# Ten products of the identity with itself on TensorE ahead of each unit's first attend, in the second of three attention stages

## The chip, the cores and the metric

The kernel runs on one core of one Trainium2 chip. The metric is the device time of one launch in microseconds; of several runs the median counts.

## The reference

Two layers on 128 sequences of 128 x 256 values. What matters here, cut from the reference:

```python
# layer 0: grouped convolutions of x and of the context, attention over 8 heads, layernorm
qh, kh, vh = _gconv(q, wq), _gconv(k, wk), _gconv(v, wv)
scores = jnp.einsum('bhdl,bhdm->bhlm', qh, kh) / sqrt(H) - 1000000000.0 * mask
...
# layer 1: self attention, cross attention with the context, feed forward
attn1 = _mha(x, x, x, look_ahead_mask, ...)
out1 = _layernorm(x + attn1, ln1_g, ln1_b)
attn2 = _mha(enc_output, enc_output, out1, padding_mask, ...)
out2 = _layernorm(out1 + attn2, ln2_g, ln2_b)
ffn = jax.nn.relu(out2 @ ffn_w1 + ffn_b1) @ ffn_w2 + ffn_b2
return _layernorm(out2 + ffn, ln3_g, ln3_b)
```

with, in each `_mha` (16 heads of depth 16),

```python
logits = jnp.einsum('bhqd,bhkd->bhqk', qh, kh) / jnp.sqrt(depth) + mask * -1000000000.0
attn = jax.nn.softmax(logits, axis=-1)
out = jnp.einsum('bhqk,bhkd->bhqd', attn, vh)
```

## The kernel before, in words

Four stages run one after the other: the convolution attention (tiles named l_), the first attention of layer 1 (mha_), the second one (mha_ too), and the feed forward (ffn_). The change touches the function `attention` (line 387), which builds the first three; its argument `phase` is 0, 1 or 2, and `PLANS[phase]` (line 52) holds the table of numbers by which each stage's work is set in slots. The second stage is `phase == 1`: 32 units (`N`) of four sequences, 512 tokens.

A unit has 16 attend steps, one for each slot, and each works on four heads of one sequence (four quads of heads for each of four sequences). In slot `i` TensorE computes, in this order (`body`, line 862):

- `attend_step(t, i)` (line 789), the first thing in each slot: four products (line 807) of keys with queries, 128 x 128 each, into `tbank[i % 2]` (banks 4 and 5 of PSUM). The operands are stacks of bf16 rows: 96 rows of split keys or queries, and three rows that carry the row maxima, so that the product comes out with the maximum of the row subtracted. For a unit's first half the maxima must have arrived before slot 0, for the second before slot 8: `max_in[0]` and `max_in[1]` are raised by the DMA that brings them.
- `pv_tile` (line 813): the probabilities of four slots times the values, 32 small-column products (line 821 in the profile) for the two slots' worth of each of four steps.
- `score_step` (line 765, products on line 775): scores of the *next* unit in the other orientation, whose only use is the row maximum. VectorE takes it (line 1076) from two banks in turn.
- the work of the table `work`: projections (line 740), values (line 759), the turn of the maxima (`max_turn`, line 780, products on line 784) and of the output (line 858).
- `output_step`, `turn_merged`, `turn_heads` (lines 852, 839, 832): the end of each sequence of the unit.

The way of the maxima: VectorE's maxima of eight score steps, GpSimd's split into three bf16 parts (line 1227), TensorE's two transposes (line 784: in slot 13 for the first half of the next unit, in slot 5 for the second half of this one), ScalarE's copy (line 924), and a DMA from ScalarE's queue into the stack (line 926). The first attend of the unit, in slot 0, waits for it.

After an attend step VectorE adds the mask in the bank (line 1091), and ScalarE takes the exponent (line 936), which frees the bank and raises `att_exp`. The attend step of slot `i` needs the exponent of slot `i - 2`:

```python
                if i % 8 == 0:
                    pe.wait_ge(max_in[i // 8], 16 * (u.u + 1))
                    if u.number() == 0 and i == 0:
                        pe.wait_ge(ones_in, ONES)
                wait(pe, att_exp, CHUNKS * u.u + i - 1)
```

All engines run orders that are written out by these tables; waits are semaphores, and each engine takes its instructions in order. `c["identb"]` is the 128 x 128 identity in bf16, made once at the start (line 312) and used as the operand of the max transposes.

Of the kernel before, what the change touches and what calls it, by code (L numbers as in the profile page):

```python
# [28 lines left out]
P = 128  # L29
# [3 lines left out]
CHUNKS = 16  # L33
# [17 lines left out]

PLANS = (
    dict(
        score=[3, 4, 5, 7, 7, 8, 10, 10, 11, 12, 12, 13, 14, 15, 16, 18],
        pv_lag=2,
        steps={'turn': 6, 'normalise': 10},
# [14 lines left out]
        split_slot=14,  # L71
    ),
    dict(
        score=[4, 6, 7, 7, 8, 9, 11, 12, 12, 13, 13, 14, 15, 15, 17, 18],
        pv_lag=2,
        steps={'turn': 6, 'turn_merged': 7, 'output': 8, 'normalise': 10},
# [16 lines left out]
        split_slot=13,  # L93
    ),
    dict(
        score=[3, 3, 5, 6, 6, 8, 9, 10, 11, 12, 12, 14, 14, 16, 17, 17],
        pv_lag=1,
        steps={'turn': 5, 'turn_merged': 7, 'output': 8, 'normalise': 9},
# [44 lines left out]
def wait(eng, sem, value):  # L143

    if isinstance(value, int) and value <= 0:
        return
    eng.wait_ge(sem, value)
# [239 lines left out]
def attention(nc, top, c, io, phase):  # L387
# [32 lines left out]
    with ExitStack() as ctx:  # L420
# [5 lines left out]
        def sem(n):  # L426
            if n not in signals:
                signals[n] = top.enter_context(nc.semaphore(f"{('even', 'odd')[phase % 2]}_{n}"))
            return signals[n]
# [62 lines left out]
        work, sbank, tbank, pvbank, fbank = bank[0:2], bank[2:4], bank[4:6], bank[6], bank[7]  # L492
# [17 lines left out]
        att_mm, att_masked, att_exp, att_pv = sem("att_mm"), sem("att_masked"), sem("att_exp"), sem("att_pv")  # L510
# [38 lines left out]
        def place(side, h):  # L549

            return 2 * h + side if conv else H * side + 2 * (h % 8) + h // 8
# [14 lines left out]
        plan = PLANS[phase]  # L566
# [146 lines left out]
        def _(pe):  # L713
# [74 lines left out]

            def attend_step(u, i):
                j, q, kt = ATT[i]  # L790
                if i % 8 == 0:
                    pe.wait_ge(max_in[i // 8], 16 * (u.u + 1))
                    if u.number() == 0 and i == 0:
                        pe.wait_ge(ones_in, ONES)
                wait(pe, att_exp, CHUNKS * u.u + i - 1)
                key = ((j // KT) * KT + kt) * P
                masked = i in plan["pe_masks"]
                if masked:
                    if u.number() == 0:
                        pe.wait_ge(c["masks_ready"], c["masks_parted"])  # L800
                    for part in range(2):
                        mask = c["mask0t_parts"][:, part, kt, (j % 2) * P:(j % 2 + 1) * P]
                        nc.tensor.matmul(tbank[i % 2][:, :].rearrange("p (s l) -> p s l", s=4), c["ident_r"][:, :],
                                         mask.unsqueeze(1).to_broadcast([P, 4, P]), start=part == 0, stop=False)
                for s in range(4):
                    h = 4 * q + s
                    mm = nc.tensor.matmul(tbank[i % 2][:, s * P:(s + 1) * P],  # L807
                                          stack[0:STACKED, u.par, place(1, h), key:key + P],
                                          stack[0:STACKED, u.par, place(0, h), j * P:(j + 1) * P],
                                          start=not masked, stop=not masked or s == 3)  # L810
                mm.then_inc(att_mm, 1)
# [50 lines left out]
            def body(t):  # L862
                for slot in range(16):
                    if exists(t, N):
                        attend_step(t, slot)
                    for at in products_in(t, slot):
                        pv_tile(*at)
                    for u, i in scores_in(t, slot):
                        score_step(u, i)
                    for u, what, step, piece, pieces in banks.in_slot(t, slot):  # L870
                        bank_ = work[banks.bank(what, step)]
                        if piece == 0:

                            wait(pe, work_out, banks.free(u, what, step))
                        if what == "project":
                            project_step(u, step, bank_, piece, pieces)
                        elif what == "values":
                            value_step(u, step, bank_, piece, pieces)
                        elif what == "max":
                            max_turn(u, step, bank_)  # L880
                        else:
                            turn_y(u, step, bank_)
                    if not conv:
                        for at in finish_in(t, slot, "output"):
                            output_step(*at)
                        for at in finish_in(t, slot, "turn_merged"):
                            turn_merged(*at)
                    for at in finish_in(t, slot, "turn"):
                        turn_heads(*at)
# [720 lines left out]
```

## Time and profile before

| | us |
|---|---|
| median of 3 runs | 4573.87 |
| the runs | 4562.73, 4573.87, 4581.44 |
| the profiled execution | 4555.99 |
| its span, first to last instruction | 4554.0 |
| TensorE busy | 4138.1 (91%) |
| VectorE busy | 3630.7 (80%) |
| ScalarE busy | 3142.2 (69%) |
| GpSimd busy | 3055.6 (67%) |
| granted TensorE clock, mean | 0.977 of 2.4 GHz |

The span begins with the first instruction and ends with the last; 2 us lie around it. A matmul's busy time in the profile has its way through the array in it, so that four products in a row, each on record with 0.22 us, take 0.24 us together. The second stage lies between about 1657 and 2766 us of the span. The granted clock is given as a share of full speed: 1.00 is 2.4 GHz, 0.50 is 1.2 GHz, and a value between is a mean over a stretch that holds both.

### The profile page before, as it was taken

The page shows a single profiled execution, that of the slowest core. Times are in us where ns is not written, and L with a number is a line of the kernel's source. Part 1 is how long each engine was busy: PE and PEld are TensorE (multiplying, and loading weights), DVE is VectorE, ACT ScalarE, POOL GpSimd, SP SyncE. Part 2 cuts the span into 40 slices and gives each one's busy share as a digit, 9 for nine tenths or more (in the row PEclk, how much of TensorE's full clock was granted, in tenths as well). Part 3 has the DMA queues.
Part 4 walks back from the last instruction along what each step waited for, and adds up shares of the span by engine and source line. Part 5 has one row for each costly group of instructions (what it writes and reads, how often), then busy time and mean ns, then how long its engine had stood idle before and what let it go on. Part 6 is the DMA issues. An engine that isn't in the chain of part 4 may idle for free. (4 is left out here: it accounts for less than half of the span.)

```text
span 4554.0 us, 131241 instructions
## 1 busy us (share of the span) xinstructions
PE 4138.1 (91%) x46088; PEld 3382.9 (74%) x46088; DVE 3630.7 (80%) x13903; ACT 3142.2 (69%) x6279; POOL 3055.6 (67%) x4630
## 2 busy tenths in 40 slices
PE   7999999999999969998999986999999997999999
PEld 5777777777777747777777764778777876999998
DVE  7898888889889858888888884777777775666666
ACT  5777777777777748777777774777777775444443
POOL 4777777777777637777777763777777773555555
PEclk9999999999999989999999997999999998999999
DMA  5444444444444435556656554667767662222221
GB/s 142 117 120 121 119 122 117 119 121 118 123 117 120 111 102 154 157 151 159 163 150 168 158 143 122 182 193 193 194 195 197 193 183 93 73 75 70 70 70 52
DMA packets 1082968, 608.89 MB, mean 134 GB/s; under 512 B 64665, under 2 KB 1082057, under 8 KB 1082313
## 3 DMA queue, kind: packets, MB, share of 16 engines
q1 hardware_dynamic: 1071896, 595.70, 47.7%
q8 instruction: 370, 6.06, 0.6%
q10 hardware_dynamic: 10416, 4.80, 0.4%
q14 instruction: 286, 2.34, 0.2%
HBM read 175.66 MB, written 117.54 MB: 64 GB/s over the span
## 5 line engine op out<-in xcount | busy, mean ns | idle before, releaser
L1076 DVE CUSTOM_DVE_ANT_0 l_junk<-l_bank,mask 128x256 bf16<-128x256 f32 x2048 | 775.4, 416 | 57.5 <-PE l_bank L775 38.1
L936 ACT ACTIVATE mha_probs<-mha_bank 128x512 f32<-128x512 f32 x1024 | 602.3, 599 | 222.6 <-DVE mha_bank L1091 114.6
L936 ACT ACTIVATE l_probs<-l_bank 128x512 f32<-128x512 f32 x1024 | 598.8, 592 | 161.8 <-DVE l_bank L1091 149.1
L1091 DVE TENSOR_TENSOR l_bank<-l_bank,mask0t 128x512 f32<-128x512 f32 x832 | 572.3, 688 | 16.5 <-PE l_bank L807 8.1
L1076 DVE CUSTOM_DVE_ANT_0 mha_junk<-mha_bank,mask 128x128 bf16<-128x128 f32 x2048 | 464.8, 284 | 45.3 <-PE mha_bank L775 44.8
L775 PE MATMUL mha_bank<-mha_stack 96*128 96x128 bf16 (+1 forms) x4096 | 373.1, 222 | 72.8 <-DVE mha_max_parts L1076 51.0
L807 PE MATMUL mha_bank<-mha_stack 99*128 99x128 bf16 (+1 forms) x4096 | 403.9, 223 | 27.8 <-DMA mha_stack<-mha_max_rows 26.4
L807 PE MATMUL l_bank<-l_stack 99*128 99x128 bf16 x4096 | 402.9, 220 | 23.9 <-ACT l_probs L936 16.2
L1445 ACT ACTIVATE ffn_hidden<-ffn_h,ffn_b_s 128x512 f32<-128x512 f32 x256 | 176.5, 689 | 356.1 <-PE ffn_h L1392 284.9
L775 PE MATMUL l_bank<-l_stack 96*128 96x256 bf16 x2048 | 374.9, 275 | 30.9 <-DVE l_max_parts L1076 25.5
L1405 PEld LDWEIGHTS ffn_o<-ffn_w_parts,ffn_hidden_parts 128*128 128x128 f32 x3072 | 384.9, 191 | 14.9 <-DVE ffn_w_parts L1516 3.5
L1091 DVE TENSOR_TENSOR mha_bank<-mha_bank,mask1t 128x512 f32<-128x512 f32 x512 | 353.6, 691 | 52.6 <-PE mha_bank L807 52.1
L1462 DVE TENSOR_TENSOR ffn_hidden_parts<-ffn_hidden,ffn_hidden_parts 128x512 fp32r<-128x512 f32 x256 | 242.1, 946 | 190.9 <-ACT ffn_hidden_parts L1445 190.6
L1405 PE MATMUL ffn_o<-ffn_w_parts,ffn_hidden_parts 128*128 128x256 f32 x3072 | 388.2, 283 | 4.7 <-DVE ffn_w_parts L1516 3.1
L1392 PE MATMUL ffn_h<-ffn_x_parts,ffn_w_parts 128*128 128x512 f32 x1536 | 374.6, 393 | 14.9 <-DVE ffn_x_parts L1457 14.3
L807 PEld LDWEIGHTS l_bank<-l_stack 99*128 99x128 bf16 x4096 | 280.4, 99 | 143.8 <-issue 83.4
L1218 POOL TENSOR_TENSOR mha_yproj<-mha_yproj,mha_parts 128x512 f32<-128x512 f32 x248 | 290.3, 1170 | 138.8 <-ACT mha_parts L909 138.6
L1067 DVE TENSOR_REDUCE mha_max_parts<-mha_bank 128x4 f32<-128x512 f32 x512 | 335.8, 681 | 36.5 <-PE mha_bank L775 34.4
L807 PEld LDWEIGHTS mha_bank<-mha_stack 99*128 99x128 bf16 (+1 forms) x4096 | 291.1, 99 | 95.0 <-DMA mha_stack<-mha_max_rows 36.6
L775 PEld LDWEIGHTS mha_bank<-mha_stack 96*128 96x128 bf16 (+1 forms) x4096 | 254.0, 98 | 140.0 <-DVE mha_max_parts L1076 63.1
L1224 POOL TENSOR_TENSOR mha_parts<-mha_yproj,mha_parts 128x512 bf16<-128x512 f32 x248 | 288.6, 1164 | 71.3 <-ACT mha_parts L978 70.3
L1392 PEld LDWEIGHTS ffn_h<-ffn_x_parts,ffn_w_parts 128*128 128x128 f32 x1536 | 282.3, 190 | 69.4 <-issue 15.7
(192 smaller groups left out, 11266.8 us busy)
## 6 DMA issues: line engine op xcount, KB each, us to landing
mha_stack<-mha_parts SPq DMA_DIRECT2D x1536, 128.0 KB, 2.9
l_stack<-l_parts SPq DMA_DIRECT2D x1024, 64.0 KB
l_stack<-l_parts SPq DMA_DIRECT2D x256, 128.0 KB
cols_o<-mha_y_t SPq DMA_DIRECT2D x128, 256.0 KB, 3.0
l_x_pad<-in_x SPq DMA_DIRECT2D x64, 256.0 KB, 3.3
l_c_pad<-in_ctx SPq DMA_DIRECT2D x64, 256.0 KB, 3.7
l_resid<-in_x_t SPq DMA_DIRECT2D x64, 256.0 KB, 3.1
cols_x<-l_y SPq DMA_DIRECT2D x64, 256.0 KB, 2.4
```

What stands on the lines that cost most here:

```text
L775: mm = nc.tensor.matmul(sbank[i % 2][:, s * KEYS:(s + 1) * KEYS], stack[0:SCORED, u.par, place(0, h), j * P:(j + 1) * P], stack[0:SCORED, ...
L807: mm = nc.tensor.matmul(tbank[i % 2][:, s * P:(s + 1) * P], stack[0:STACKED, u.par, place(1, h), key:key + P], stack[0:STACKED, u.par, pla ...
L936: nc.scalar.activation(probs[:, i % RING, :], tbank[i % 2][:, :], ACT.Exp).then_inc(att_exp, 1)
L1067: nc.vector.tensor_reduce(max_parts[:, j, 0, col:col + SH * GROUPS - 1:GROUPS], sbank[i % 2][:, :].rearrange("p (s k) -> p s k", s=SH), op ...
L1076: ins = nc.vector.tensor_tensor_reduce(out=junk[:, i % 2, cols], in0=sbank[i % 2][:, cols], in1=mask, scale=1.0, scalar=LOWEST, op0=ALU.ad ...
L1091: nc.vector.tensor_tensor(bank_, bank_, mask.unsqueeze(1).to_broadcast([P, 4, P]), ALU.add).then_inc(att_masked, 1)
L1218: nc.gpsimd.tensor_tensor(rest, rest, parts[:, u.par, i, HI, :], ALU.subtract).then_inc(rest_step, 1)
L1224: nc.gpsimd.tensor_tensor(parts[:, u.par, i, LO, :], rest, parts[:, u.par, i, MID, :], ALU.subtract).then_inc(split_done, 1)
L1392: mm = nc.tensor.matmul(hbank[f % 4][:, :], w1_parts[:, a, kt, f * P:(f + 1) * P], x_parts[:, u.par, b, kt, :], start=(i == 0), stop=(i == 5))
L1405: mm = nc.tensor.matmul(obank[j][:, 0:L], hidden_parts[:, u.par, b, f, j * P:(j + 1) * P], w2_parts[:, a, f, :], start=(f == 0 and i == 0) ...
L1445: last = nc.scalar.activation(out, hbank[f % 4][:, :], ACT.Relu, bias=c["ffn_b1_s"][:, f:f + 1])
L1462: nc.vector.tensor_tensor(hidden_parts[:, u.par, 1, f, :], hidden[:, f % 2, :], hidden_parts[:, u.par, 0, f, :], ALU.subtract).then_inc(h_ ...
```

## The change

The plan of each stage gets an entry `rehearsals`, a pair: how many extra products stand ahead of the attend step in slot 0 and in slot 8. It is (10, 0) in the second stage and (0, 0) in the others. Each product is the bf16 identity (stationary) with the bf16 identity (moving), 128 columns, written into the bank that the attend step fills right after. It goes to the four column groups of the bank in turn. The attend's products overwrite all of it, so no result uses them. The wait for the exponent that frees the bank moves ahead of the extra products, and with that ahead of the wait for the maxima, in all three stages.

```diff
@@ -71,6 +72,7 @@
     dict(
+        rehearsals=(10, 0),
         score=[4, 6, 7, 7, 8, 9, 11, 12, 12, 13, 13, 14, 15, 15, 17, 18],
@@ -788,11 +791,14 @@
             def attend_step(u, i):
                 j, q, kt = ATT[i]
+                wait(pe, att_exp, CHUNKS * u.u + i - 1)
                 if i % 8 == 0:
+                    for n in range(plan["rehearsals"][i // 8]):
+                        nc.tensor.matmul(tbank[i % 2][:, (n % 4) * P:(n % 4 + 1) * P], c["identb"][:, :],
+                                         c["identb"][:, :], start=True, stop=True)
                     pe.wait_ge(max_in[i // 8], 16 * (u.u + 1))
                     if u.number() == 0 and i == 0:
                         pe.wait_ge(ones_in, ONES)
-                wait(pe, att_exp, CHUNKS * u.u + i - 1)
                 key = ((j // KT) * KT + kt) * P
```

In TensorE's order, at the boundary between the first and the second unit of the second stage (last rows of slot 15, then slots 0 and 1), there stands before:

```order
L858 MATMUL mha_bank<-ident,mha_z 128x128
L839 MATMUL mha_bank<-ident,mha_merged 128x128 [waits odd_merged_done]
L839 MATMUL mha_bank<-ident,mha_merged 128x128
L807 MATMUL mha_bank<-mha_stack 128x128 [waits odd_att_exp,odd_max_in0]
L807 MATMUL mha_bank<-mha_stack 128x128 x3
L858 MATMUL mha_bank<-ident,mha_z 128x128 [waits odd_normed,odd_work_out]
L858 MATMUL mha_bank<-ident,mha_z 128x128
L852 MATMUL mha_bank<-mha_wo,mha_merged_t 128x256 [waits odd_mt_out]
```

and with the change, at the same place (three lines further down in the code up to the attend step, six behind it: 807 is now 813, 858 is 864, 839 is 845, 852 is 858):

```order
L864 MATMUL mha_bank<-ident,mha_z 128x128
L845 MATMUL mha_bank<-ident,mha_merged 128x128 [waits odd_merged_done]
L845 MATMUL mha_bank<-ident,mha_merged 128x128
L797 MATMUL mha_bank<-identb 128x128 [waits odd_att_exp]
L797 MATMUL mha_bank<-identb 128x128 x9
L813 MATMUL mha_bank<-mha_stack 128x128 [waits odd_max_in0]
L813 MATMUL mha_bank<-mha_stack 128x128 x3
L864 MATMUL mha_bank<-ident,mha_z 128x128 [waits odd_normed,odd_work_out]
```

The ten products of line 797 stand between the end of the old unit and the first attend, and the one row that waited for two semaphores is now two rows that wait for one each. This piece comes 31 times; in the first unit of the stage the ten have no wait. Nothing else moves on any engine.

## Rows read from the trace of the kernel before

**Rows 1.** Page, 40 equal slices of the span: granted TensorE clock in tenths.

```profile
PEclk9999999999999989999999997999999998999999
```

**Rows 2.** Stretches of stages 2 and 3: length, busy time (instructions) by engine, clock, DMA.

```profile
1700.00:2735.00 1035.00, 943.45 (x10907) 753.61 (x10905) 894.63 (x5051) 804.21 (x1612) 745.01 (x1032) 0.96 0.59 156
2834.00:3799.00 965.00, 894.04 (x11478) 763.62 (x11477) 752.74 (x1665) 727.24 (x1441) 726.56 (x806) 1.00 0.67 186
```

**Rows 3.** Waits of TensorE, 1685 to 2780 us: total us, times, longest.

```profile
PE mha_bank L807 <- DMA mha_stack<-mha_max_rows: 21.7, 29, 1.9
```

**Rows 4.** Timeline of TensorE at one boundary: start, us, instruction, [idle before it, releaser].

```profile
2019.24 0.29 PE L784 MATMUL mha_bank<-identb,mha_max_parts 128*48 128x128 bf16 x2
...
2020.79 0.40 PE L775 MATMUL mha_bank<-mha_stack 96*128 96x128 bf16 x4 [0.92 <-DVE mha_max_parts L1076]
...
2022.67 0.40 PE L775 MATMUL mha_bank<-mha_stack 96*128 96x128 bf16 x4 [0.60 <-DVE mha_max_parts L1076]
...
2023.75 0.44 PE L839 MATMUL mha_bank<-ident,mha_merged 128*128 128x128 f32 x2 [0.45 <-DVE mha_merged L1129]
2025.05 0.61 PE L807 MATMUL mha_bank<-mha_stack 99*128 99x128 bf16 x4 [0.86 <-DMA mha_stack<-mha_max_rows]
2025.45 0.64 PE L858 MATMUL mha_bank<-ident,mha_z 128*128 128x128 f32 x2
2025.88 1.92 PE L852 MATMUL mha_bank<-mha_wo,mha_merged_t 128*128 128x256 f32 x4
```

**Rows 5.** Half-microsecond stretches at two boundaries; the clock stands third from the end.

```profile
1816.50:1817.00 0.50, 0.50 (x5) 0.15 (x2) 0.50 (x2) 0.34 (x1) 0.50 (x2) 0.64 1.32 273
...
2024.50:2025.00 0.50, 0.00 (x0) 0.00 (x0) 0.50 (x7) 0.50 (x3) 0.50 (x1) 0.85 1.19 263
2025.00:2025.50 0.50, 0.45 (x5) 0.46 (x6) 0.38 (x4) 0.31 (x1) 0.50 (x2) 0.50 1.21 266
```

**Rows 6.** Stretches from line 784 in slot 13 to line 784 in slot 5.

```profile
1714.76:1730.33 15.57, 13.09 (x166) 10.57 (x164) 14.02 (x82) 11.32 (x23) 13.04 (x17) 1.00 0.47 128
...
1812.65:1830.71 18.06, 15.77 (x167) 12.11 (x165) 14.21 (x82) 11.88 (x24) 12.84 (x17) 0.81 0.82 217
...
1915.53:1933.25 17.72, 15.90 (x166) 12.19 (x164) 14.03 (x82) 11.72 (x24) 13.01 (x17) 0.81 0.85 217
...
2019.24:2036.58 17.34, 14.49 (x166) 11.53 (x164) 14.14 (x82) 11.63 (x24) 13.01 (x17) 0.90 0.87 217
...
2088.41:2104.28 15.87, 13.01 (x167) 10.51 (x165) 14.12 (x82) 11.60 (x24) 13.03 (x17) 1.00 0.87 219
...
2459.79:2475.36 15.57, 13.05 (x166) 10.52 (x164) 13.67 (x81) 11.39 (x24) 13.03 (x17) 1.00 0.84 225
2492.26:2510.22 17.96, 15.78 (x166) 12.10 (x164) 14.12 (x82) 11.71 (x24) 13.01 (x17) 0.81 0.84 218
...
2594.92:2610.91 15.99, 14.42 (x166) 11.50 (x165) 14.03 (x82) 11.62 (x24) 13.03 (x17) 0.89 0.87 227
...
2660.71:2677.80 17.09, 14.61 (x167) 11.47 (x165) 14.03 (x82) 11.71 (x24) 13.01 (x17) 0.90 0.93 213
```

**Rows 7.** Timeline of TensorE at the boundaries after 2088.41 and after 2459.79.

```profile
2094.22 0.40 PE L807 MATMUL mha_bank<-mha_stack 99*128 99x128 bf16 x4 [0.89 <-DMA mha_stack<-mha_max_rows]
...
2464.77 0.40 PE L807 MATMUL mha_bank<-mha_stack 99*128 99x128 bf16 x4
2465.01 0.39 PE L858 MATMUL mha_bank<-ident,mha_z 128*128 128x128 f32 x2
...
2473.08 1.13 PE L852 MATMUL mha_bank<-mha_wo,mha_merged_t 128*128 128x256 f32 x4 [0.51 <-ACT mha_merged_t L947]
```

**Rows 8.** Timeline of ScalarE at the boundary of rows 4: the exponent of slot 14.

```profile
2022.40 0.58 ACT L936 ACTIVATE mha_probs<-mha_bank 128x512 f32<-128x512 f32 x1
```

**Rows 9.** Max transposes, 1690 to 2750 us: min/median/max ns of one, first and last start.

```profile
L784 PE MATMUL mha_bank<-identb,mha_max_parts x126: 219/228/239, 1696.5 to 2742.1; 128*48 128x128 bf16 x126
```

More of the change, by code:

```diff
@@ L53 @@
     dict(
+        rehearsals=(0, 0),
         score=[3, 4, 5, 7, 7, 8, 10, 10, 11, 12, 12, 13, 14, 15, 16, 18],
@@ L95 @@
     dict(
+        rehearsals=(0, 0),
         score=[3, 3, 5, 6, 6, 8, 9, 10, 11, 12, 12, 14, 14, 16, 17, 17],
```

## The prediction

> **What bounds the kernel now.** I began with the clock line of the page's 40 slices [rows 1]. The granted TensorE clock is full nearly everywhere but in the slices around the changes of stage and in a few others, so the question is where the rest of the loss sits. Stretches of whole stages answer it [rows 2]: over 1035 us of the second stage the granted clock is 0.96, over 965 us of the third it is 1.00. TensorE is busy 943.45 of the 1035 us, more than any other engine (VectorE 894.63), and the unit is mostly a TensorE chain. The waits of TensorE in that stage [rows 3] name 21.7 us, 29 times, in which the four products of line 807 waited for the DMA that brings the row maxima: that is the first attend of a unit.
>
> The timeline of one boundary shows the place [rows 4]. From the max transposes at 2019.24 (line 784, slot 13 of the unit before) TensorE works in crumbs: it sits idle 0.92, 0.60 and 0.45 us for VectorE, then 0.86 us for the DMA, and the first attend starts at 2025.05. Just there the clock goes from 1.00 over 0.85 to 0.50, 2.4 to 1.2 GHz [rows 5]. What follows is the densest work of the unit and runs at half rate: the attend's four products take 0.40 us to the next row, where the same four take 0.24 us at a clean boundary (2464.77 to 2465.01, [rows 7]), and line 852 stands with 1.92 us.
>
> I cut the stage at line 784: each unit has one stretch from slot 13 to slot 5 of the next unit, holding the boundary, and one from slot 5 to slot 13, which measures 16.91 us at most units. The 29 stretches with a boundary between 1714.76 and 2677.80 are of two kinds [rows 6]. Ten have clock 1.00 and last 15.57 to 16.00 us, sum 157.1, mean 15.71. Nineteen have a clock of 0.81 to 0.91 and last 15.99 to 18.39 us, sum 330.6, mean 17.40. Rows 6 give the first and the last and one of each sort; the others repeat them. So a dip of the clock costs 17.40 - 15.71 = 1.69 us, and 19 of them cost 32 us.
>
> **The change, part by part.**
> - *Ten products, 128 columns, bf16, in front of each first attend of stage 2: 32 units, 320 products and 320 weight loads.* A like product costs (2465.01 - 2464.77) / 4 = 0.06 us at the full clock [rows 7] and 0.40 / 4 = 0.10 us at half [rows 4]. So ten cost 0.6 us, or 1.0 us in a dip. They need bank 4 free, which the exponent of slot 14 frees: it starts at 2022.40 and lasts 0.58 us [rows 8], before line 839 at 2023.75 is even issued. They can start when line 839's two transposes are issued, about 0.22 us after their start, at 2023.97 or 4.73 us after line 784, and end at 5.3 us. The DMA released the attend 5.81 us after line 784 here and at 2094.22 - 2088.41 = 5.81 in a clean unit [rows 7]. There the products lie wholly in the wait and cost nothing.
> - *Where the maxima come early.* In the clean unit at 2459.79 the attend started at 4.98. The products push it to 5.3. But that unit had 0.51 us to wait later, at line 852 for ScalarE (2473.08), and its attend-to-slot-5 part took 10.59 us, where the unit at 2088.41 with its late attend took 2104.28 - 2094.22 = 10.06. A first attend up to 15.57 - 10.06 = 5.5 us after line 784 is therefore free. Cost 0; if that cover were gone, 0.3 us in some ten units, 3 us. With the products at half clock the end is 4.73 + 1.0 = 5.7, 0.2 us too late.
> - *The wait for the exponent moved ahead of the wait for the maxima,* in all three stages and in every step. TensorE needed both before its first attend anyway; in the other stages nothing stands between them. Cost 0: nothing is queued between the two. ScalarE, VectorE, GpSimd and all DMA queues keep their orders.
> - *What is gained.* If the 0.6 us of products turns the crumbs into enough work to hold the clock, a dipped boundary becomes a clean one. Upper value 19 x 1.69 = 32 us. Lower value: the unit of rows 4 has its attend at 5.81 and would last 10.06 + 5.81 = 15.87 instead of 17.34, 1.47 us, x 19 = 28 us. I take 30 us.
> - *What stays.* Four of the 19, those at 1812.65, 1915.53, 2492.26 and 2594.92, are of another sort: their clock falls 3.4 to 4.1 us after line 784, before the place of the products (the first of them between 1816.5 and 1817.0, [rows 5]), and three of them lose twice as much clock, 0.81 instead of 0.90. They exceed the clean mean by 18.06 + 17.72 + 17.96 + 15.99 - 4 x 15.71 = 6.9 us [rows 6]. I leave 7 us of loss.
> - *Sum* against the profiled execution (4555.99 us, span 4554.0): 30 - 7 = 23 us less, 4533. The median of the three runs shown is 17.9 us above the profiled one, and these four times span 4556 to 4581. Ten clean boundaries turned into dips would be 10 x 1.69 = 17 us, so this spread may well be dips that the profiled run was spared and that the change would remove too; or it has another cause, and stays. I count a third of it, 6 us: 4573.87 - 23 - 6 = 4545.
>
> Is more work at this place what holds the clock? The rows say so only by contrast: the clean unit of rows 7 at 2459.79 had the same VectorE waits and differs in that its last wait is short (attend at 4.98, not 5.81); yet the unit at 2088.41 was as late as that of rows 4 and stayed clean. So the crumbs are near the limit, and which side a boundary falls on depends also on when it comes. That is good for a remedy of 0.6 us in 5.8, and bad for certainty.
>
> **The rivals.**
> 1. *The products do not hold the clock.* For: the products are ten times the same small thing, and no row shows such a stream. Then the dips stay, the products hide in the wait or end 0.2 us late in the 19: 0 to +4 us, 4574 to 4578. The Trainium skill ("TensorE: Matmul & The Clock Gate", section "Why this matters for your kernels") ties the fall to a long gap in which the engine does nothing between bursts, and by that rule products in a gap that is short anyway are worth nothing, which is this rival's time. The trace speaks against the rule as it stands: ahead of the fall at 2024.5 to 2025.0 no gap is over 0.92 us. Chance 0.20.
> 2. *The dips move.* The dipped stretches stand together, twice five in a row; clean units are 1.7 us shorter, so with the dips gone the boundaries come at other times, and more of them may fall as the four above did, ahead of the products. If half of 31 did at 6.9 / 4 = 1.7 us each, 27 us would come back: 4574 - 30 + 27 = 4571. Chance 0.14.
> 3. *The products themselves are the wait* (the other side). They sit in TensorE's in-order stream ahead of the attend; VectorE's mask, ScalarE's exponent and everything behind line 807 wait for them. The point from which they decide is 5.5 us after line 784, so at more than (5.5 - 4.73) / 10 = 0.08 us each. They write four column groups in turn, so the fifth meets the first. If each took the 0.22 us that a lone one has on record [rows 9], they would end at 6.9 us, 1.4 us too late: 31 x 1.4 = 43 us, and 43 - 0 with the dips staying gives 4617, 43 - 30 with them gone 4587. Against it: rows of four products, and the 32 of line 821, pass at 0.06 us and less. Chance 0.06, of which 0.04 for over 0.5% slower.
>
> That the change does nothing of what it says I exclude: the order of TensorE shows the ten products in 32 units, ahead of the wait for the maxima.
>
> **How the numbers follow.** Forecast (clock held at most boundaries) 0.60, rivals 0.20, 0.14, 0.06. A measurement of this kernel can tell about 0.5%, 23 us: faster means below 4551. Within the forecast the gain runs from 15 us (half of the dips left) to 32 + 17 = 49, that is 4559 to 4525; 0.55 of its 0.60 lies below 4551, which is faster. Same: the rest of the forecast, rivals 1 and 2, and the part of rival 3 that ends at 4587, 0.05 + 0.20 + 0.14 + 0.02 = 0.41. Slower (over 4597): 0.04. The range goes from 4522 (all of it gained) to 4578 (rival 1 with its delay), which leaves out rival 3 and the far ends.
>
> **What would show it.** Right: in the profile after, ten products of line 797 in some 0.6 us ahead of each first attend; a granted clock of 0.98 to 0.99 over stage 2; most boundary stretches at 15.6 to 15.9 us with clock 1.00, and few dips, those beginning before the products; the wait of the attend for the maxima down from 0.7 to about 0.3 us; slot 5 to slot 13 still 16.9. Wrong: the stretches still at 17.2 with clock 0.90 (rival 1), dips in as many units but earlier (rival 2), attends starting later than 5.9 us after the max transposes with no DMA wait (rival 3).

## The result, and the profile after

| | before | after |
|---|---|---|
| median, 6 runs each (us) | 4570.79 | 4546.45 |
| lowest and highest (us) | 4562.73 to 4581.44 | 4542.55 to 4555.10 |
| profiled execution (us) | 4555.99 | 4551.44 |
| TensorE busy (us) | 4138.1 | 4143.9 |
| granted clock, mean | 0.977 | 0.979 |

The ratio of the runs is 0.995, 95% interval 0.9934 to 0.9966. (Of the experiments below, one of e1's ten executions took 5502 us at a mean granted clock of 0.68 and is left out of its ratio.) That is 0.5% faster, right on the bound that the prediction set for "faster", and a ratio of 1 lies outside the interval. Two later measurements bracket it: the change once more gave 0.9962 (0.9950 to 0.9975), and a variant that keeps the old order of the waits elsewhere 0.9940 (0.9924 to 0.9956).

The stretch of stage 2 and the wait of the first attend, from the stretches and from the waits of TensorE (1685 to 2780 us) of the kernel after; they answer to [rows 2, 3]:

```profile
1700.00:2735.00 1035.00, 949.88 (x11333) 769.78 (x11329) 903.74 (x5074) 810.39 (x1627) 749.20 (x1042) 0.98 0.60 156
...
PE mha_bank L813 <- DMA mha_stack<-mha_max_rows: 14.4, 22, 1.2
```

The clock of stage 2 rose from 0.96 to 0.98, and the wait for the maxima fell from 21.7 us, 29 times, to 14.4 us, 22 times, since the products now fill its start. The same boundary as in [rows 4], in the timeline of TensorE after:

```profile
2015.78 0.29 PE L787 MATMUL mha_bank<-identb,mha_max_parts 128*48 128x128 bf16 x2
...
2020.29 0.44 PE L845 MATMUL mha_bank<-ident,mha_merged 128*128 128x128 f32 x2 [0.45 <-DVE mha_merged L1135]
2020.57 0.72 PE L797 MATMUL mha_bank<-identb 128*128 128x128 bf16 x10
2021.88 0.40 PE L813 MATMUL mha_bank<-mha_stack 99*128 99x128 bf16 x4 [0.60 <-DMA mha_stack<-mha_max_rows]
2022.12 0.39 PE L864 MATMUL mha_bank<-ident,mha_z 128*128 128x128 f32 x2
2022.34 1.03 PE L858 MATMUL mha_bank<-mha_wo,mha_merged_t 128*128 128x256 f32 x4
```

The ten products start 4.79 us after the max transposes and are followed by a wait of 0.60 us for the DMA, so they cost nothing here. Line 858, which was line 852, takes 1.03 us instead of 1.92: the clock is full. The boundary stretches, cut as in [rows 6], the first and the last of 29 and those the text speaks of:

```profile
1714.75:1730.31 15.56, 13.38 (x177) 11.10 (x175) 14.09 (x82) 11.32 (x23) 13.03 (x17) 1.00 0.46 125
...
1779.97:1797.66 17.69, 15.11 (x177) 12.18 (x175) 14.12 (x82) 11.59 (x24) 13.01 (x17) 0.90 0.93 212
...
1880.92:1897.80 16.88, 14.74 (x177) 12.33 (x175) 14.21 (x82) 11.67 (x24) 13.05 (x17) 0.90 0.82 211
...
2015.78:2031.93 16.15, 13.56 (x177) 11.11 (x175) 14.14 (x82) 11.62 (x24) 13.00 (x17) 1.00 0.86 218
...
2181.93:2198.39 16.46, 14.90 (x177) 12.40 (x175) 14.12 (x82) 11.59 (x24) 13.00 (x17) 0.90 0.96 220
...
2444.55:2462.96 18.41, 16.40 (x176) 13.04 (x174) 13.81 (x81) 11.73 (x24) 12.96 (x17) 0.81 0.96 212
...
2647.45:2663.38 15.93, 13.56 (x177) 11.11 (x175) 14.12 (x82) 11.57 (x24) 13.01 (x17) 1.00 0.95 217
```

Eight of the 29 are dipped, where 19 were; the sum of all 29 is 473.3 us, where it was 487.7. In five of the eight the clock falls 3.4 to 4.1 us after the max transposes, ahead of the products. One of these, at 2181.93, in half-microsecond stretches and in the timeline:

```profile
2185.00:2185.50 0.50, 0.16 (x2) 0.17 (x3) 0.50 (x6) 0.50 (x2) 0.50 (x1) 0.85 1.09 387
2185.50:2186.00 0.50, 0.50 (x6) 0.47 (x4) 0.50 (x2) 0.50 (x2) 0.50 (x2) 0.50 1.09 365
```

```profile
2186.89 1.27 PE L797 MATMUL mha_bank<-identb 128*128 128x128 bf16 x10
2187.96 0.63 PE L813 MATMUL mha_bank<-mha_stack 99*128 99x128 bf16 x4
```

There the products run at half clock, 2187.96 - 2186.89 = 1.07 us, and the attend waits for them and not for the DMA. In the other three dips the clock falls after the products, at boundaries whose maxima came late (the attend starts 5.98 to 6.65 us after the max transposes). A late attend alone does not decide it: the clean stretches after have attends up to 6.40 us.

### The profile page after: what moved, and what is told of

The parts are those of the page before. It is cut to its first block and busy times, and to the rows that moved or that the text cites. A ratio compares the mean times of both kernels' runs of the same rounds, so it can differ in the third digit from the quotient of the medians.

```text
span 4549.4 us, 131850 instructions
## 1 busy us (share of the span) xinstructions
PE 4143.9 (91%) x46408; PEld 3398.4 (75%) x46408; DVE 3633.0 (80%) x13903; ACT 3138.6 (69%) x6279; POOL 3050.0 (67%) x4630
```

## The experiments

All ratios are to the kernel before, timed beside the experiment; "dipped" counts the same 29 stretches in the experiment's profile, "early" those whose clock falls within 4.1 us of the max transposes. All but e9 are edits of the kernel after.

| run | what | ratio (95%) | dipped (early) | sum of 29, us |
|---|---|---|---|---|
| first profile before | | 1 | 19 (4) | 487.7 |
| e9 | kernel before, again | 0.9995 (0.9982 to 1.0008) | 22 (5) | 502.5 |
| e1 | only the wait moved | 1.0019 (1.0006 to 1.0033) | 20 (4) | 501.5 |
| e2 | ten products of 2 columns | 1.0006 (0.9992 to 1.0020) | 21 (6) | 504.8 |
| e4 | ten ahead of slot 8 | 1.0013 (0.9999 to 1.0027) | 20 (6) | 503.7 |
| e10 | five products | 0.9970 (0.9958 to 0.9982) | 14 (5) | 488.8 |
| after | the change | 0.9950 (0.9934 to 0.9966) | 8 (5) | 473.3 |
| e5 | the change, again | 0.9962 (0.9950 to 0.9975) | 7 (6) | 473.1 |
| e11 | the change, order of waits kept | 0.9940 (0.9924 to 0.9956) | 6 (4) | 472.0 |
| e3 | five fp32 transposes | 0.9945 (0.9926 to 0.9963) | 7 (5) | 472.6 |
| e8 | twenty products | 0.9990 (0.9978 to 1.0001) | 17 (17) | 488.2 |
| e7 | products in the three earlier gaps | 0.9946 (0.9932 to 0.9959) | 1 (0) | 467.6 |
| e6 | products in all four gaps | 0.9934 (0.9921 to 0.9946) | 0 | 463.6 |
| e12 | e6, order of waits kept | 0.9918 (0.9904 to 0.9932) | 0 | 467.1 |

### e1: only the order of the waits

```diff
-        rehearsals=(10, 0),
+        rehearsals=(0, 0),
```

> No extra products; only the wait for the exponent stands ahead of the wait for the maxima, as in the change. Theory (the products hold the clock): the same as the kernel before, ratio 0.998 to 1.002, some 17 to 22 of the 29 boundary stretches dipped. Rival (the order of the waits gives the gain): ratio near 0.995 with about 8 dipped.

20 dipped, as expected, and no gain: the order of the waits is not where the change's gain comes from. The ratio of 1.0019 even lies above 1 with its whole interval; e11 and e12 come back to it.

### e2: the same instructions, two columns each

```diff
-nc.tensor.matmul(tbank[i % 2][:, (n % 4) * P:(n % 4 + 1) * P], c["identb"][:, :],
-                 c["identb"][:, :], start=True, stop=True)
+nc.tensor.matmul(tbank[i % 2][:, (n % 4) * P:(n % 4) * P + 2], c["identb"][:, :],
+                 c["identb"][:, 0:2], start=True, stop=True)
```

> Ten products at the same place, but each moves 2 columns of the identity instead of 128; the ten weight loads of 128 columns stay. Theory that the columns streamed hold the clock: the dips come back, 15 or more of 29, ratio 0.998 to 1.002. Rival, that any ten instructions on TensorE there (or their delay, or the weight loads) do it: about 8 dipped, ratio near 0.995.

The dips are back, 21 of 29. A boundary in the timeline of TensorE:

```profile
2024.36 0.44 PE L845 MATMUL mha_bank<-ident,mha_merged 128*128 128x128 f32 x2 [0.46 <-DVE mha_merged L1135]
2024.64 0.39 PE L797 MATMUL mha_bank<-identb 128*128 128x2 bf16 x10
2027.10 0.61 PE L813 MATMUL mha_bank<-mha_stack 99*128 99x128 bf16 x4 [2.07 <-DMA mha_stack<-mha_max_rows]
```

The ten products and their ten loads of 128 columns are there, but over in 0.39 us from first start to last end (0.72 us for the change's ten, counted the same way), and the attend behind them runs at half clock (0.61 us). This attend is the latest of the run; the other late falls stand at boundaries with attends from 5.36 us on. Ten instructions, or ten weight loads, are not enough.

### e3: transposes in place of products

```diff
-        rehearsals=(10, 0),
+        rehearsals=(5, 0),
...
-nc.tensor.matmul(tbank[i % 2][:, (n % 4) * P:(n % 4 + 1) * P], c["identb"][:, :],
-                 c["identb"][:, :], start=True, stop=True)
+nc.tensor.transpose(tbank[i % 2][:, (n % 4) * P:(n % 4 + 1) * P], c["ident"][:, :],
+                    c["ident"][:, :])
```

> In place of the ten products five fp32 transposes of the identity, about the same 0.6 us of TensorE. Theory that busy columns count whatever the mode: about 8 dipped of 29 as in the change, ratio near 0.995. Rival, the page's rule that transposes do not count as busy in the same way: 15 or more dipped, ratio near 1.000.

7 dipped and 0.9945: five fp32 transposes do what ten bf16 products do. A clean boundary of e3:

```profile
2080.38 0.71 PE L797 MATMUL mha_bank<-ident 128*128 128x128 f32 x5
2080.92 0.39 PE L813 MATMUL mha_bank<-mha_stack 99*128 99x128 bf16 x4
```

Five transposes move 5 x 128 columns in 2080.92 - 2080.38 = 0.54 us. The five bf16 products of e10 move as many columns in about 0.28 us and leave 14 dips. With the same number of columns, then, the work that took twice as long left half the dips. The Trainium skill says of transposes ("TensorE: Matmul & The Clock Gate", section "Part 4: PE-mode transpose") that they don't count as busy in the same way and don't bring the full clock. For fp32 transposes in this kernel the measurement goes against the first half of this. They stood among other products, at a clock that was already full; whether transposes alone would bring the full clock, no run here shows.

### e4: the ten products at a dense place

```diff
-        rehearsals=(10, 0),
+        rehearsals=(0, 10),
```

> The ten products stand ahead of the attend of slot 8 instead of slot 0, where TensorE has no gap in the trace before. Theory: they cost their full 0.56 us in each of 32 units, 18 us, and the dips of the boundary stay as before (17 to 22 of 29); ratio 1.003 to 1.005, the stretch from slot 5 to slot 13 grows from 16.9 to 17.45 us. Rival, that products anywhere in a unit help: ratio below 1.000 and few dips.

20 dipped, so products elsewhere in the unit do nothing for the boundary. The price was expected wrong. The stretch from slot 5 to slot 13 grew from 16.90 us to 17.08, not to 17.45:

```profile
1804.91 0.72 PE L797 MATMUL mha_bank<-identb 128*128 128x128 bf16 x10
1805.47 0.39 PE L813 MATMUL mha_bank<-mha_stack 99*128 99x128 bf16 x4
1805.70 0.39 PE L778 MATMUL mha_bank<-mha_stack 96*128 96x128 bf16 x4
1805.92 1.08 PE L858 MATMUL mha_bank<-mha_wo,mha_merged_t 128*128 128x256 f32 x4
```

The products take 1805.47 - 1804.91 = 0.56 us, but line 858 comes just behind, and in the kernel before it (as line 852) had a short wait there for ScalarE's copy of the merged heads, which ends at 1801.47. The same place before, in the unit whose stretch begins at 1795.73:

```profile
1801.12 0.40 PE L775 MATMUL mha_bank<-mha_stack 96*128 96x128 bf16 x4
1801.52 1.13 PE L852 MATMUL mha_bank<-mha_wo,mha_merged_t 128*128 128x256 f32 x4
```

There 0.40 us lie between the two starts, and 0.22 us in e4: 0.18 us of the 0.56 goes into that wait. The four products of the line itself are 0.05 us shorter, and the second such step of the stretch, which started 14.08 us into it before and 14.27 in e4, takes up some 0.14 us more. A place with no gap in front of it still had small ones behind it.

### e5 and e6: the change again, and products in all four gaps

e6 adds, to the change, 12 products in the first gap of [rows 4], 8 in the second and 10 in the third:

```diff
+                    if fills and slot == 14:
+                        pe.wait_ge(att_exp, CHUNKS * t.u + 14)
+                        rehearse(tbank[1], 12)
+                    for n, (u, i) in enumerate(scores_in(t, slot)):
+                        if fills and slot == 15 and n == 1 and 8:
+                            wait(pe, work_out, banks.free(t, "turn_y", 0))
+                            rehearse(work[banks.bank("turn_y", 0)], 8)
                         score_step(u, i)
...
+                        if fills and slot == 15:
+                            pe.wait_ge(att_exp, CHUNKS * t.u + 15)
+                            rehearse(tbank[0], 10)
                         for at in finish_in(t, slot, "turn_merged"):
                             turn_merged(*at)
```

> The change as it is, to stand beside the others on one chip. Theory: ratio 0.994 to 0.996 to the kernel before; in its profile 6 to 11 of the 29 boundary stretches dipped, most of them with a fall 3 to 4 us after the max transposes.

> Products of the identity in all four gaps of the boundary: 12 behind the attend of slot 14 (into the bank that slot 13's exponent has freed), 8 between the two score steps of slot 15 (into the work bank of the next turn), 10 ahead of the merged turn, and the 10 of the change. Theory: no dip at any boundary, all 29 stretches at 15.55 to 16.3 us, 8 x 1.3 = 10 us less than the change, ratio 0.991 to 0.993. Rival (products in these gaps push TensorE's chain back): stretches of 16.5 us and more at clock 1.00, no better than the change.

e5 repeats the change: 7 dipped, 6 of them early, sum 473.1. In e6 no stretch is dipped. One boundary in its timeline, and then its longest stretch:

```profile
2012.39 0.29 PE L787 MATMUL mha_bank<-identb,mha_max_parts 128*48 128x128 bf16 x2
2012.61 0.40 PE L813 MATMUL mha_bank<-mha_stack 99*128 99x128 bf16 x4
2012.85 0.83 PE L821 MATMUL mha_bank<-identb 128*128 128x128 bf16 x12
2013.93 0.40 PE L778 MATMUL mha_bank<-mha_stack 96*128 96x128 bf16 x4 [0.25 <-DVE mha_max_parts L1097]
...
2015.06 0.61 PE L821 MATMUL mha_bank<-identb 128*128 128x128 bf16 x8
2015.82 0.40 PE L778 MATMUL mha_bank<-mha_stack 96*128 96x128 bf16 x4
...
2016.28 0.72 PE L821 MATMUL mha_bank<-identb 128*128 128x128 bf16 x10
2016.90 0.44 PE L850 MATMUL mha_bank<-ident,mha_merged 128*128 128x128 f32 x2
2017.17 0.72 PE L797 MATMUL mha_bank<-identb 128*128 128x128 bf16 x10
2017.79 0.40 PE L813 MATMUL mha_bank<-mha_stack 99*128 99x128 bf16 x4
```

```profile
2407.53:2424.75 17.22, 15.13 (x206) 12.85 (x205) 14.12 (x82) 11.60 (x24) 12.98 (x17) 1.00 0.83 209
```

The score step that VectorE released 2020.79 - 2019.24 = 1.55 us after the transposes before is released at 1.54 us now: the products push nothing back. Sum 463.6 us, 9.7 less than the change, as expected. The ratio of 0.9934 is a little short of the 0.991 to 0.993 expected. Its interval overlaps that of the first measurement of the change, but not that of e5 (0.9950 to 0.9975), which was measured together with it. e5's own ratio of 0.9962 lies just above the 0.994 to 0.996 expected. The stretch of 17.22 us has full clock; its maxima came 7.17 us after the transposes. The expected upper end was 16.3, and six of the 29 stretches exceed it, all with attends from 6.31 us on. The DMA itself is issued 0.76 to 0.87 us after the max transposes at each of the 29 boundaries, in e6 as in the kernel before, so what varies lies between its issue and its landing. That is what is left of the boundary: not the clock but the DMA.

### e7: the three earlier gaps alone

```diff
-        rehearsals=(10, 0),
+        rehearsals=(0, 0),
```

on top of e6.

> The products in the three earlier gaps (12, 8 and 10), and none in the wait for the maxima. Theory: the three gaps matter together more than the last one: a handful of dips at most (0 to 6 of 29), ratio 0.992 to 0.995. Rival (only work right ahead of the first attend counts): 15 or more dipped.

One dip, sum 467.6, ratio 0.9946. Products ahead of the attend are not needed if the gaps before are filled: it is work in the whole thin stretch that holds the clock, and not only what stands right ahead of the attend. (e7 has 30 products for each unit where the change has ten, so it does not show that the earlier gaps are the better place for the same ten.)

### e8: twenty products

```diff
-        rehearsals=(10, 0),
+        rehearsals=(20, 0),
```

> Twenty products instead of ten ahead of the first attend; they end at 4.76 + 20 x 0.056 = 5.9 us after the max transposes. The point from which a late attend costs is 5.5, the maxima land at 5.3 to 6.6. Theory: the dips with a fall after 5 us go (3 of 29), those with a fall at 3 to 4 us stay or become more (5 or more); early boundaries pay 0.4 us; together no better than the change: ratio 0.994 to 0.997. Rival (more products, fewer dips): under 3 dipped, ratio 0.992.

The ratio is 0.9990, worse than the 0.994 to 0.997 expected. No late fall is left, but 17 early ones are there, far more than the handful that "5 or more" had in mind. Of the 29 stretches, a clean one and four that follow each other:

```profile
1852.06:1867.98 15.92, 13.94 (x187) 11.67 (x185) 14.12 (x82) 11.63 (x24) 13.02 (x17) 1.00 0.89 223
...
1919.18:1936.39 17.21, 15.34 (x186) 12.90 (x185) 14.12 (x82) 11.63 (x24) 13.00 (x17) 0.90 0.87 218
1953.30:1970.58 17.28, 15.38 (x186) 12.89 (x184) 14.25 (x82) 11.68 (x24) 13.00 (x17) 0.90 0.90 218
1987.48:2004.68 17.20, 15.35 (x186) 12.80 (x184) 14.12 (x82) 11.63 (x24) 12.99 (x17) 0.90 0.95 219
2021.61:2038.82 17.21, 15.35 (x187) 12.88 (x185) 14.14 (x82) 11.62 (x24) 12.99 (x17) 0.90 0.86 219
```

This is rival 2 of the prediction, and it needs twenty products to come true. In a unit with an early fall the twenty run at half clock, 2028.73 - 2026.60 = 2.13 us in the timeline, and put the attend at 7.1 us, behind nearly any landing of the maxima:

```profile
2026.60 2.34 PE L797 MATMUL mha_bank<-identb 128*128 128x128 bf16 x20
2028.73 0.43 PE L813 MATMUL mha_bank<-mha_stack 99*128 99x128 bf16 x4
```

Such a unit lasts 34.1 to 34.2 us (1919.18 to 1953.30, and so on), and the next one falls early again, each of the four shown 3.8 us after its max transposes. So when a boundary comes matters too, as the prediction suspected. The clean stretch gives the price of the late attend at full clock: the products end at 5.87 us, the stretch takes 15.92 where 15.56 is the least, 0.36 us, which is what the prediction's free point of 5.5 us asks for.

### e9: the kernel before, again

> The kernel before, unchanged, for a second profile of it. In the first one the attend of slot 0 came 5.59 us after the max transposes on average (29 boundaries); with the moved wait alone (e1) it came at 5.99, and the 29 stretches were 501.5 us instead of 487.7. If the first profile was a lucky one (landing times differ from run to run): about 6.0 here, 20 dips, 500 us. Rival (the order of the waits delays the maxima): 5.6 and 488 us again, and a ratio of 1.000 against e1's 1.002.

22 dipped, the attend at 5.93 us on average, sum 502.5: the first profile was a lucky one. Three of its stretches, the last with an early fall:

```profile
1811.47:1831.05 19.58, 15.51 (x167) 12.09 (x165) 14.27 (x82) 11.87 (x24) 12.82 (x17) 0.83 0.84 200
...
2015.85:2033.36 17.51, 14.60 (x166) 11.51 (x165) 14.14 (x82) 11.70 (x24) 12.97 (x17) 0.90 0.86 221
...
2154.98:2173.12 18.14, 15.57 (x166) 12.09 (x165) 14.12 (x82) 11.71 (x24) 12.96 (x17) 0.81 0.94 212
```

Its profiled execution took 4576.11 us, 20.1 more than the first; 14.8 of these lie in the 29 stretches. Another 8.9 lie behind them: from the end of the last stretch to the end of the span it took 1885.1 us, where the first profile took 1876.2. The part ahead of the stretches was 3.5 us shorter.

The early falls show something that the count of dips hides. Without the ten products they mostly lose the full clock for twice as long: their stretches have a mean clock of about 0.81 in 23 of 25 cases (3 of 4 in the first profile, 4 of 5 in e9, all 16 in e1, e2 and e4), and last 17.7 to 18.5 us. With ten products or five transposes it is 5 of 20 (the change 1 of 5, e5 4 of 6, e11 0 of 4, e3 0 of 5); the other 15 have 0.90 and last 16.4 to 16.9 us. The five have attends from 6.49 us on, the 15 at 6.03 to 6.25; without the products an attend at 5.38 us was too late. So the products, though they stand behind an early fall, bring the full clock back sooner where the maxima are not very late. That is read from counts; no run was made to test it alone.

### e10: five products

> Five products instead of ten ahead of the first attend. Theory (what counts is busy time in the thin stretch): some of the late falls stay, 9 to 16 of 29 dipped, ratio 0.996 to 0.999. Rival (any plain product there is enough): as the change, 7 or 8 dipped, ratio 0.995 to 0.996.

14 dipped, between 22 and 8, and the ratio lies between too. The early falls (5) are as many as ever; of the late ones 9 are left, where 17 are in e9 and 3 in the change. The products at full clock:

```profile
2115.97 0.44 PE L797 MATMUL mha_bank<-identb 128*128 128x128 bf16 x5
```

They last 0.44 us from first start to last end, not much more than the 0.39 us of e2's ten, which held nothing. The effect grows with the amount of work.

### e11 and e12: the order of the waits kept

Both keep the order of the kernel before in every step without extra products:

```diff
-                wait(pe, att_exp, CHUNKS * u.u + i - 1)
                 if i % 8 == 0:
+                    if plan["rehearsals"][i // 8]:
+                        wait(pe, att_exp, CHUNKS * u.u + i - 1)
...
+                if i % 8 or not plan["rehearsals"][i // 8]:
+                    wait(pe, att_exp, CHUNKS * u.u + i - 1)
```

> The change with the wait for the exponent moved only where the ten products stand; in every other step the waits keep the order of the kernel before. If the moved wait costs (e1: ratio 1.0019, interval 1.0006 to 1.0033): 6 to 9 us better than the change, ratio 0.993 to 0.995. If e1's excess was chance: 0.995 to 0.997 as the change.

> Products in all four gaps (e6) with the order of the waits kept as before elsewhere. Theory: no dips in the 29 stretches, ratio 0.992 to 0.994 as e6; if the order of the waits costs, 0.990 to 0.992.

e11 came where it was expected if the moved wait costs, e12 too. e11 is 0.0022 below e5, e12 is 0.0016 below e6, and e1 is 0.0019 above the kernel before: three times the same sign and size, some 8 us. But e5 and e6 were measured on another chip than e11 and e12, each against the kernel before on its own, the intervals of e11 and e5 and of e12 and e6 overlap, e1's overlaps that of the unchanged kernel in e9, and no profile shows a place where the time would lie (e12's 29 stretches are even 3.5 us longer than e6's, by later maxima). Whether the order of the two waits costs 0.2% stays open. e12 has the lowest ratio of all, 0.8% below the kernel before; its interval overlaps that of e6.

## Why the prediction was right, and where it was not

- **The bound, and the way of the gain.** Right. Dipped boundaries went from 19 (22 in e9) to 8 (7 in e5, 6 in e11), and e1, e2, e3, e4 and e10 leave no other cause than work that streams columns through TensorE in the thin stretch. Rival 1 fell: work in gaps of under a microsecond holds the clock, and e6 has no fall at all. The Trainium skill ("TensorE: Matmul & The Clock Gate", section "Why this matters for your kernels") ties the fall to a long gap, and that does not account for the falls here, as the prediction said from its trace.
- **The price of the products.** "End at 5.3 us", "0.06 us each": measured 4.76 to 5.32 us at full clock at most boundaries, 0.056 us each. The free point of 5.5 us was met by e8 (0.36 us for 5.87 us). Rival 3 fell.
- **The upper value, 1.69 us for each dip.** About right. From e9 to the change the sum of the 29 fell by 29.2 us with 14 dips less, 2.1 us for each; from the first profile it fell by 14.4 with 11 less, 1.3 for each. The two differ by the landings, below.
- **What stays.** Forecast were the four early dips. There were five, about as many as in the kernel before (4 and 5): rival 2 did not come true with ten products. Not forecast were two things: the three late falls at late maxima, and that four of the five early falls cost little (clock 0.90, 16.45 to 16.88 us), since the full clock came back sooner.
- **The signs.** The clock of stage 2 and the length from slot 5 to slot 13 (16.89 us) came as forecast. "Most boundary stretches at 15.6 to 15.9" did not: 11 of 29 are clean and no longer than 15.93 us, and ten more are clean at 16.03 to 16.47. The attend's wait for the maxima, over the 29 boundaries alone (24 of the 29 waits of [rows 3], and 18 of the 22 after), went from a mean of 0.61 us to 0.36.
- **The step that failed: the sum against the profiled execution.** It said 4533 us; the profiled execution after took 4551.4. The 29 stretches gave 14.4 us, not 23. Clean stretches were taken at 15.71 us, their mean in the first profile, and measured 15.96 after, because the maxima landed later: the attend came at 5.96 us on average, where it was 5.59. That is not the change's doing, as e9 has 5.93 without it. Over 29 stretches it makes 7 us; the eight dips exceed the clean mean by 10.5 us together, where 7 was left for them. The rest, 14.4 - 4.6 = 9.8 us, was lost behind the last of these stretches, where the change has two more boundaries and, in stage 3, the moved wait. ScalarE's first rounding of stage 3 is 12.3 us earlier than before, the first feed-forward product 6.6 us, the end 4.6 us. Most of this is again the luck of the first profile: from the last stretch to the end it took 1876.2 us, the change 1886.0, and e9, the unchanged kernel, 1885.1.
- **The step that made up for it: the median's excess.** Of the 17.9 us by which the median lay above the profiled execution a third was counted. e9 shows that most of such an excess is in stage 2 (14.8 of 20.1 us), and so within the reach of the change. So two errors of opposite sign gave 4545 where 4546.45 was measured. A third helped: the forecast took 29 us from 4573.87, the median of three; the median of six is 4570.79, and the gain between the medians is 24.3 us. The mechanism carried the prediction; its closeness to 2 us is luck.
- **The chances.** 0.55 for over 0.5% faster, 0.41 within: the measurement, at 0.5%, could not decide between them either.

## What to carry to other kernels

Where TensorE is the bound and its clock falls at the same place of every unit, look at the crumbs ahead of the fall: small gaps that each have a good reason can together cost the dense work behind them half its speed. Products of a constant with itself fill such gaps for nothing, as long as they end before the releaser they wait beside and write a bank that is free; fill all the gaps of the thin stretch a little instead of the last one fully, since too many in one gap (e8) make a dipped unit longer and the dips repeat. Take a second profile of the kernel before when the profiled execution lies off the median: here its first profile hid half of the effect.

## What the runs showed of the hardware

- Instructions and weight loads alone did not hold the clock, streaming columns did. Ten products with full weight loads but two columns each took 0.39 us from first start to last end and held nothing (21 dipped); ten with 128 columns (0.72 us), or five fp32 transposes (0.71 us), took the dips to 7 or 8; five products (0.44 us) to 14. The transposes move as many columns as the five products, in twice the time.
- After an early fall, stretches with the products behind it had a mean clock of 0.90 in 15 of 20 cases; without them it was about 0.81 in 23 of 25.
- fp32 transposes, among other products, held the clock as products did (e3, 7 dipped), against the Trainium skill's sentence on transposes cited at e3.
- The first attend, which waits for the same 24 KB of maxima, started on average 5.59 us after the transposes that precede it in one execution of the kernel before and 5.93 in another, and up to 7.17 us after them in e6, though the DMA is issued within 0.87 us of them each time. At full clock a stretch lasts about 10.06 us more than that start, and never under 15.54. With the clock full everywhere, this is the longest wait that is left at the boundary; it was not tried to shorten it.
